# The experts' second product in bfloat16 halves, and expert numbers fetched four at a time

## The reference, cut to what matters

```
logits = einsum('btd,ed->bte', x, Wr); probs = softmax(logits)
topk_vals, topk_idx = top_k(probs, 2)
router_weights = topk_vals / topk_vals.sum(-1)
h = silu(x @ W1[e].T)        # W1: 8 x 512 x 128
y = h @ W2[e].T              # W2: 8 x 128 x 512
out = sum over the two experts of gate * y
```

## Time and profile before

| | |
|---|---|
| median of 3 executions | 565.09 us (564.62 to 568.42) |
| the profiled execution | 566.33 us |
| its span in the trace | 564.5 us |
| first expert stage, hidden(0) to the last outputs | 267.8 to 366.6 us |
| second expert stage | 450.0 to 546.6 us |
| TensorE matmul busy | 488.1 us (86%) |
| VectorE, ScalarE, GpSimd busy | 292.4, 250.6, 247.5 us |

### The profile page before, as it was taken

The page is one execution under the profiler, slowest core; times in us unless marked ns, Lnnn a source line. Parts: engine busy times, 40 slices in busy tenths (PEclk is TensorE's granted clock), DMA queues, the critical chain, the costliest instruction groups (busy, mean ns, idle before and its releaser), DMA issues.

```text
span 564.5 us, 12563 instructions
## 1 busy us (share of the span) xinstructions
PE 488.1 (86%) x4071; PEld 378.0 (67%) x4071; DVE 292.4 (52%) x960; ACT 250.6 (44%) x529; POOL 247.5 (44%) x229
## 2 busy tenths in 40 slices
PE   1989999999999999899979999937998499999970
PEld 0647776868666887766867787715777297787750
DVE  5556495948796789746731010057577743010115
ACT  7754566573645444333322323346663122232333
POOL 7134262435332464641676253621146567343460
PEclk9998898999898999989889999969998679999995
DMA  7865292967396337011132310040001223311007
GB/s 234 255 145 82 61 171 63 171 135 104 86 148 134 66 95 130 15 34 39 39 87 82 82 35 24 36 149 2 1 19 40 66 68 82 86 53 35 21 30 224
DMA packets 66594, 48.36 MB, mean 86 GB/s; under 512 B 7861, under 2 KB 60615, under 8 KB 66534
## 3 DMA queue, kind: packets, MB, share of 16 engines
q1 hardware_dynamic: 61430, 36.99, 30.8%
q0 software_dynamic: 5104, 10.57, 5.3%
HBM read 16.14 MB, written 27.59 MB: 77 GB/s over the span
## 4 chain that ended last, share of the span: by engine, by line
PE 70%; DVE 11%; issue 6%; DMA 5%; POOL 3%; SPq 2%; ACT 2%; POOLq 0%; DVEq 0%; ACTq 0%
PE PS L817 14%; PE PS L658 9%; PE PS L801 7%; PE PS L803 4%; PE PS L645 3%; PE PS L710 3%; PE PS L620 3%; PE PS L802 3%; PE PS L639 3%; PE PS L556 2%; DMA X<-in_x 2%; PE PS L602 2%; PE PS L668 2%; PE PS L629 2%; SPq L303 2%
## 5 line engine op out<-in xcount | busy, mean ns | idle before, releaser
L507 POOL DMA_INDIRECT YY<-W2R,ID x78 | 77.0, 988 | 81.4 <-ACT W2R L1296 62.8
L451 POOL TENSOR_TENSOR R<-NM,I64B 128x1024 bf16<-128x1024 f32 x32 | 61.4, 1920 | 114.0 <-DVE NM L1464 109.0
L1288 ACT ACTIVATE W2R<-PS 128x512 f32<-128x512 f32 x78 | 46.6, 597 | 125.9 <-PE PS L803 125.8
L817 PE MATMUL PS<-WB,W2R 128*128 x624 | 90.5, 291 | 0.0
L495 POOL DMA_INDIRECT XS<-W1R,SLOT x64 | 64.0, 1000 | 48.0 <-DVE SLOT L1590 31.4
L801 PE MATMUL PS<-QKM,WA 128*128 128x128 bf16 x312 | 71.7, 232 | 9.6 <-issue 4.4
L817 PEld LDWEIGHTS PS<-WB,W2R 128*128 128x128 f32 x624 | 77.8, 197 | 2.4 <-issue 0.2
L1741 DVE COPY QKM<-PS 128x1024 bf16<-128x1024 bf16 (+1 forms) x20 | 13.5, 677 | 123.6 <-PE PS L780 123.6
L803 PE MATMUL PS<-QKM,WA 128*128 128x128 bf16 x312 | 71.7, 232 | 0.0
L802 PE MATMUL PS<-QKM,WA 128*128 128x128 bf16 x312 | 69.5, 225 | 0.0
L658 PEld LDWEIGHTS PS<-VB,PF 128*128 128x128 f32 x512 | 60.1, 193 | 9.2 <-issue 9.2
(11 more groups left out here) (207 smaller groups left out, 871.2 us busy)
## 6 DMA issues: line engine op xcount, KB each, us to landing
XS<-CST SPq DMA_DIRECT2D x30, 520.0 KB, 9.9
QKM<-XS SPq DMA_DIRECT2D x78, 65.0 KB
QKM<-QK SPq DMA_DIRECT2D x64, 72.0 KB, 2.1
QKM<-YY SPq DMA_DIRECT2D x16, 256.0 KB, 4.8
W2R<-in_W POOLq DMA_DIRECT2D x1, 2048.0 KB, 12.3
YY<-W2R,ID POOLq DMA_INDIRECT x78, 2.2
XS<-CST SPq DMA_DIRECT2D x2, 585.0 KB, 9.0
XS<-W1R,SLOT POOLq DMA_INDIRECT x64
```

Of the source, the lines that this page charges most:

```text
L451: nc.gpsimd.tensor_tensor(R[:, u % 2], NM[:, u % 2].unsqueeze(2).to_broadcast([P, NH, WIN]), I64B[:].unsqueeze(1).to_broadcast([P, NH, WIN ...
L507: pool.indirect_dma_start(out=YY[f], out_offset=to, in_=YS[n % NY][:, i, :], in_offset=None, bounds_check=NPAIRS - 1, oob_is_err=False) \
L817: last = mm(o, HF[n % 3][:, k, :], WB[:, e, k, :].rearrange("p o c -> p (o c)"), start=k == 0, stop=k == KF - 1)
L1288: fn(HF[n % 3], PS[:, n % 3, :].rearrange("p (k s) -> p k s", k=KF), ACT.Silu).then_inc(s["f_hf"], 1)
```

## The change

The hidden activations are split into a bfloat16 high half and the bfloat16 rest, and the weights WB likewise, as two halves of each 128 columns beside each other. For each of the four k, `outputs(t)` makes one product of the high activations with both halves of the weights (256 columns, the two results beside each other in PSUM), and one of the low activations with the high weights, added onto the first 128 columns. The two halves of the result are added when PSUM is copied out.

- ScalarE's `silu(t)` becomes two: SiLU to float32 (HF, now two buffers) and SiLU again to bfloat16 (high half of HB).
- VectorE gets `low(t)`: HF less the high half, to the low half of HB, for every tile.
- `y_out` moves from ScalarE to VectorE: a sum over pairs of PSUM values 128 columns apart. It runs on 2 tiles at a time, the last three tiles singly, since a bank now holds 2 tiles; YS has 8 buffers of 2 tiles in place of 4 of 4. It is called at the head of `low(t)` for the pair that ended with tile t-2.
- `choose` loads the four expert numbers of a group at once, ahead of the group, and without the instructions that hold the value against its bounds.
- VectorE gets `second_lo(e)` in block A: the low half of each of the eight WB weights, at the end of the units of `W2_STEPS`. What waited for ScalarE's copy to WB now waits for VectorE's.
- In the first stage the sends of the fourth sequence stand behind two pairs of results, in the second still ahead of all.
- `route_gates` on VectorE now stands behind the stage's last `y_out`; `route_table` of the second phase stands behind turned(1) and low(2) in the second stage, where it was ahead of route_place.

```diff
-NY = 4
+NY = 8
...
+YGROUPS = [list(range(g, g + 2)) for g in range(0, NTILE - 3, 2)] + [[g] for g in range(NTILE - 3, NTILE)]
...
-        WB = sb("WB", [P, NE, KF, D])
+        WB = sb("WB", [P, NE, KF, 2, D], BF16)
...
-                    if y == 1 - f:
+                    if y == 2 - 2 * f:
                         dispatch(f, B - 1)
...
-                def choose(t):
+                def choose(g):
+                    tiles = GROUPS[g]
                     for i, (_, t0, _) in enumerate(PHASES):
-                        if t == t0:
+                        if tiles[0] == t0:
                             pe.wait_ge(s["f_table"], 2 * (NPH * f + i + 1))
-                    which[t] = pe.value_load(EID[0:1, t:t + 1], min_val=0, max_val=NE - 1)
+                    _, experts_of = nc.values_load_multi_w_load_instructions(
+                        EID[0:1, tiles[0]:tiles[-1] + 1], engines=[mybir.EngineType.PE], min_val=0, max_val=NE - 1,
...
-                    pe.wait_ge(s["f_hf"], n + 1)
+                    pe.wait_ge(s["f_hl"], n + 1)
...
-                        last = mm(o, HF[n % 3][:, k, :], WB[:, e, k, :].rearrange("p o c -> p (o c)"), start=k == 0,
-                                  stop=k == KF - 1)
+                        hh, hl = (HB[n % 3][:, h, k, :] for h in range(2))
+                        mm(o, hh, WB[:, e, k, :, :].rearrange("p o h c -> p (o h c)"), start=k == 0, stop=False,
+                           skip_group_check=True)
+                        last = mm(o[:, 0:D], hl, WB[:, e, k, 0, :].rearrange("p o c -> p (o c)"), start=False,
+                                  stop=k == KF - 1, skip_group_check=True)
...
                     if t < NTILE and t % 4 == 2 + late and t // 4 + 1 < NGRP:
                         turned(t // 4 + 1)
+                        if not late:
+                            choose(t // 4 + 1)
                     if t >= 2:
                         outputs(t - 2)
-                    if t + 1 < NTILE:
-                        choose(t + 1)
+                    if t < NTILE and t % 4 == 3 and late:
+                        choose(t // 4 + 1)
...
+                    if n >= 2:
+                        act.wait_ge(s["f_hl"], n - 1)
+                    fn(HF[n % 2], z, ACT.Silu).then_inc(s["f_hf"], 1)
                     if n >= 3:
                         act.wait_ge(s["f_y"], n - 2)
-                    fn(HF[n % 3], PS[:, n % 3, :].rearrange("p (k s) -> p k s", k=KF), ACT.Silu).then_inc(s["f_hf"], 1)
...
+                    fn(HB[n % 3][:, 0], z, ACT.Silu).then_inc(s["f_hf"], 1)
...
+            def second_lo(e, bank):
+                dve.wait_ge(s["wt_hi"], NE + e + 1)
+                hi, lo = (WB[:, NE - 1 - e, :, c, :] for c in range(2))
+                v.tensor_tensor(lo, PS[:, bank, :].rearrange("p (k d) -> p k d", d=D), hi, ALU.subtract) \
+                    .then_inc(s["wt_lo"], 1)
...
+                def y_out(*last):
+                    for y in (y for y, tiles in enumerate(YGROUPS) if tiles[-1] in last):
+                        m, w = f * len(YGROUPS) + y, len(YGROUPS[y])
+                        dve.wait_ge(s["f_y"], f * NTILE + YGROUPS[y][-1] + 1)
...
+                        halves = PS[:, 4 + m % 2, 0:2 * w * D].rearrange("p (t h d) -> p t d h", h=2, d=D)
+                        v.tensor_reduce(YS[m % NY][:, 0:w, :], halves, op=ALU.add, axis=AXX).then_inc(s["f_ys"], 1)
+
+                def low(*tiles):
+                    for t in tiles:
+                        n = f * NTILE + t
+                        y_out(t - 2)
+                        dve.wait_ge(s["f_hf"], 2 * n + 2)
+                        if n >= 3:
+                            dve.wait_ge(s["f_y"], n - 2)
+                        v.tensor_tensor(HB[n % 3][:, 1], HF[n % 2], HB[n % 3][:, 0], ALU.subtract).then_inc(s["f_hl"], 1)
...
                 for g in range(3, NGRP):
+                    late = GROUPS[g][0] in [t0 for _, t0, _ in PHASES]
+                    low(*range(4 * g - 4, 4 * g - 2 + late))
                     turned(g)
                     identities(g)
+                    low(*range(4 * g - 2 + late, 4 * g))
```

More of the change, by code:

```diff
@@ L64 @@
 NGRP = len(GROUPS)
-YGROUPS = [list(range(g, g + 4)) for g in range(0, NTILE - 7, 4)] \
-    + [list(range(g, g + 2)) for g in (NTILE - 7, NTILE - 5)] + [[g] for g in range(NTILE - 3, NTILE)]
+YGROUPS = [list(range(g, g + 2)) for g in range(0, NTILE - 3, 2)] + [[g] for g in range(NTILE - 3, NTILE)]
 XROW = D + 2
@@ L249, in program @@
               for c in range(B)]
+        hb = qkm[:, 14592:14592 + 3 * 2 * DFF].rearrange("p (i h k s) -> p i h k s", i=3, h=2, k=KF)
+        HB = [hb[:, i] for i in range(3)]
         w2r = W2R[:].rearrange("p e f -> p (e f)")
         HF = [w2r[:, 512 * i:512 * i + 512].rearrange("p (k s) -> p k s", k=KF) for i in range(3)]
-        YS = [w2r[:, 1536 + 512 * i:1536 + 512 * i + 512].rearrange("p (t d) -> p t d", d=D) for i in range(NY)]
+        YS = [w2r[:, 1536 + 256 * i:1536 + 256 * i + 256].rearrange("p (t d) -> p t d", d=D) for i in range(NY)]
         XR = [XZ[:]] * B, [x[:, 0:2].rearrange("p j k d -> p (j k) d") for x in YL]
@@ L697, in hidden_a @@
                 if f == 1 and b == 0:
-                    pe.wait_ge(s["wt_hi"], NWT)
+                    pe.wait_ge(s["wt_lo"], NWT)
                 if f == 1 and b == 1:
@@ L783, in experts @@
                 which = {}
-                def choose(t):
+                def choose(g):
+                    tiles = GROUPS[g]
                     for i, (_, t0, _) in enumerate(PHASES):
-                        if t == t0:
+                        if tiles[0] == t0:
                             pe.wait_ge(s["f_table"], 2 * (NPH * f + i + 1))
-                    which[t] = pe.value_load(EID[0:1, t:t + 1], min_val=0, max_val=NE - 1)
+                    _, experts_of = nc.values_load_multi_w_load_instructions(
+                        EID[0:1, tiles[0]:tiles[-1] + 1], engines=[mybir.EngineType.PE], min_val=0, max_val=NE - 1,
+                        skip_runtime_bounds_check_because="a count of at most NE experts, clamped to 1 and less 1")
+                    which.update(zip(tiles, experts_of))
                 def hidden(t):
@@ L795, in hidden @@
                     if n >= 3:
-                        pe.wait_ge(s["f_hf"], n - 2)
+                        pe.wait_ge(s["f_hf"], 2 * (n - 2))
                     xh, xl = (FHL[g % 3][:, h, t % 4 * P:t % 4 * P + P] for h in range(2))
@@ L882, in beside @@
                     if c == 1:
-                        pe.wait_ge(s["wt_hi"], NE + 4)
+                        pe.wait_ge(s["wt_lo"], NE + 4)
                     if c >= 3:
@@ L888, in beside @@
                     if c == 1:
-                        pe.wait_ge(s["wt_hi"], NE + 6)
+                        pe.wait_ge(s["wt_lo"], NE + 6)
                     if c >= 2:
@@ L906, in beside @@
                     else:
-                        pe.wait_ge(s["wt_hi"], NE + 1)
+                        pe.wait_ge(s["wt_lo"], NE + 1)
                     select(c + 1, 0, 0, 5)
@@ L911, in beside @@
                     if c == 1:
-                        pe.wait_ge(s["wt_hi"], NE + 7)
+                        pe.wait_ge(s["wt_lo"], NE + 7)
                     if c >= 2:
@@ L1122, in weights_hi @@
                 act.wait_ge(s["wt_ps"], i + 1)
-                o = WB[:, NE - 1 - e].rearrange("p k d -> p (k d)") if second else WA[:, 0, NE - 1 - e, :]
-                fn(o, PS[:, bank, :], ACT.Copy).then_inc(s["wt_hi"], 1)
+                o = WB[:, NE - 1 - e, :, 0, :] if second else WA[:, 0, NE - 1 - e, :].rearrange("p (k d) -> p k d", d=D)
+                fn(o, PS[:, bank, :].rearrange("p (k d) -> p k d", d=D), ACT.Copy).then_inc(s["wt_hi"], 1)
             def padded(dst, src, name, **how):
@@ L1304, in experts @@
                         route_x_t(f, B - 1)
-                    for y, tiles in enumerate(YGROUPS):
-                        if tiles[-1] == t - 2:
-                            y_out(y)
-                for y, tiles in enumerate(YGROUPS):
-                    if tiles[-1] > NTILE - 3:
-                        y_out(y)
                 act.wait_ge(s["f_lg"], (f + 1) * B)
@@ L1691, in beside @@
                     input_variance(c + 2)
+                for e, bank in W2_STEPS.get((c, t), ()):
+                    second_lo(e, bank)
             dve.wait_ge(s["ld_x"], 16)
@@ L1763, in experts @@
                     route_variance(f, c)
+                    low(0)
                     identities(0)
                     route_normalised(f, c)
+                    low(1)
                     route_split(f, c)
                     turned(1)
+                    low(2)
                     identities(1)
                     route_table(f, 1)
+                    low(3)
                     route_choose(f, c)
+                    low(4)
                     route_place(f, c)
+                    low(5)
                     turned(2)
```

(14 more changed lines are left out.)

18 lines of the change are left out of this document (7 added, 11 removed).

## The result

| | before | after |
|---|---|---|
| median of 4 executions each | 564.86 us (561.84 to 568.42) | 546.61 us (545.96 to 553.01) |
| the profiled execution | 566.33 us | 546.39 us |
| its span in the trace | 564.5 us | 544.6 us |
| TensorE, VectorE, ScalarE busy | 488.1, 292.4, 250.6 us | 453.9, 371.5, 275.9 us |

The ratio is 0.97, with an interval of 0.9608 to 0.9792. The change saves 18.25 us of the median and 19.9 us of the span. The prediction's sum was 26.6 us in the trace, a third too large, and its 27 us of the median was half too large. Direction and range held.

The account below looks back on a forecast made before the run. TensorE was taken to set the pace, its instruction queue limiting hidden and its array the outputs. First stage -14.0, second -15.6, block A +3 gave -26.6 us in the trace, hence a 538 us median; range 525 to 553.

Parts of the forecast that it names:

- Steady part: Second expert stage and first alike: a group of four tiles falls from 9.6 to 6.96 us, saving 15.2 and 19.2 us.
- the term for the outputs: Outputs of each tile: counted at 0.54 us by TensorE's queue, though the array needs 0.70; 2.16 us per group.
- The range from 0.30 to 0.84 for a load: Expert-number load on TensorE's queue, once per group: lower bound 0.30 us, upper 0.84, taken as 0.6.
- The array as the bound: Rival for the expert stages: the array, not the queue, limits; a group takes 6.06 us, total 526.5 us; chance 0.12.
- The queue gains nothing: Rival: a k's second product costs the queue 0.12 us, like one with an address; total 560 to 568 us; chance 0.07.
- VectorE as the bound: Rival: sends stretch low to 2.31 us, so VectorE needs 2.9 us a tile; total 599 us; chance 0.05.
- up to double: y_out on VectorE: reading pairs 512 bytes apart might cost up to double the 0.34 us a tile.
- Block A: Eight new VectorE subtractions: three in units 7 to 9, plus waits ahead of them, cost +3 us, bounds 0 and 7.
- The sign that I had named: Block A, unit 9: TensorE's transposes would wait longer for XZ in the changed kernel's profile.
- Heads: Start of each expert stage: later sends cost +1.2 us in the first, outputs(7) waiting for low(7) +3.6 in the second.
- The ends: From last hidden to last send of each stage: old and new paths equal within 0.3 us, counted as 0.

Follow-up runs that it names:

- e1: The kernel before with only the load of four expert numbers at once, float32 outputs and no low or second_lo: 530.08 us, ratio 0.9382.
- e2: The changed kernel with the earlier load, one expert number per tile and with its bounds instructions: 579.5 us, ratio 1.029.
- e5: The kernel before with one load per tile as before, but without its two bounds instructions: 543.31 us, ratio 0.9607.
- e4: The changed kernel with expert 0's first weights for all tiles, so hidden has no address instructions: 529.63 us in one run.
- e3: The changed kernel with each second_lo one unit later on VectorE, behind the next unit's context and maxima: 536.66 us, ratio 0.9507.
- e9: The kernel before with one load per four tiles, the fourth sequence's sends ahead of results, and expert 0's weights in hidden: 523.97 us in one run.
- e8: The changed kernel with second_lo one unit later, low(7) ahead of third-phase route_table, and first-stage fourth-sequence sends ahead of all results: 534.36 us, ratio 0.947.

## Why the prediction was right, and its size wrong

**Steady part: right in kind, 5.9 us too large.** Tiles 16 to 38 were to save 22 x 2.4 x 0.275 = 14.5 us in each stage and saved 11.6 and 11.5. The step that failed is "what the array still has to do while the queue goes on is made up there; I count by the queue, 0.54". Outputs took 0.64, the array's pace, hidden behind them 1.06 in place of 1.02, and transposes and load 0.76 in place of 0.72: 0.40, 0.16 and 0.04 more in a group of four, 0.6 in all, so the term for the outputs is the one that was sized wrong. By the same count the queue had only 0.1 of lead over the array at the end of the outputs, and hidden with its address instructions didn't make it up. Why part of the tiles has a further gap of 0.1 to 0.2 between hidden and outputs isn't settled.

**What the gain comes from: not asked.** The sum took products and load together. By the queue alone the outputs cost 4 x 0.12 = 0.48 in float32 and 0.54 in bfloat16: in that count the products bring nothing, and all of the gain is the load's. The prediction had both numbers and didn't put them beside each other. e1 and e2 show it: 53.0 to 40.7 with the load alone, 53.5 with the products alone. The range from 0.30 to 0.84 for a load was sound, and e5 splits it: 0.31 a tile for the bounds.

**The array as the bound** (rival at 0.12) didn't come true, and e4 shows why: 5.8 us a group, under the 6.06 given, but only without the address instructions of hidden. **The queue gains nothing**: its premise, 0.12 for the second product of a k, is refuted: the weight load of L826 starts 0.01 to 0.07 behind that of L824 in 294 of 312 cases, and four more products a tile cost e2 only 0.02 us a tile (53.5 against 53.0). And yet for the products as such its result is the true one (e2).

The Trainium skill's rule of about 62 ns for every MATMUL with hardware decode off (TensorE: Matmul & The Clock Gate, section Wait — 56ns, not 53.3ns?) would have made a group 9.0 by the prediction's estimate. The trace has 7.5, and in e4 the products of hidden start 0.05 to 0.06 us apart, so that rule doesn't set the pace here. The 0.11 to 0.13 us of a product with an address instruction do: without them in hidden a group falls to 5.8.

**VectorE as the bound** (0.05) is refuted. low and y_out in the change, ns min/median/max:

```profile
L1767 DVE TENSOR_TENSOR QKM<-W2R,QKM x78: 678/682/693, 275.4 to 524.4; 128x512 bf16<-128x512 f32 x78
```

```profile
L1758 DVE TENSOR_REDUCE W2R<-PS x42: 415/691/693, 285.3 to 526.1; 128x256 f32<-128x512 f32 x36, 128x128 f32<-128x256 f32 x6
```

No low was stretched among 78, of which 53 overlap a send in time. In the same trace three of the eight subtractions to HL took 2.30 us in place of 0.73, as in the earlier trace rows. The sum over pairs 512 bytes apart costs 0.69, as the reduce in order of the earlier trace rows, not up to double. By the Trainium skill (SBUF — State Buffer, section Who interferes with whom) a VectorE instruction with two SBUF inputs is held by a GpSimd instruction that reads SBUF; here indirect sends from SBUF didn't hold one.

**Block A: right in kind, too low in size, and mostly elsewhere.** I had +3 from "three subtractions plus the waits ahead of them" in units 7 to 9. e3 puts it at 8 us to unit 17, and the largest waits are elsewhere: six waits of 15.6 us in all, the longest at the end of unit 6, ahead of the maxima of unit 7, the next at the end of unit 13, and only 1.6 us of them at the end of units 7 and 8. The sign that I had named, TensorE waiting longer for XZ, didn't come: that wait of 0.40 us is absent in the change. I priced the instruction, not the wait that the whole of VectorE's list stands behind.

```profile
DVE WB L1406 <- ACT WB L1135: 15.6, 6, 5.4
```

Why the table above has only +4.3: units 17 to 30 took 87.2 us in place of 89.9, at a granted clock of 1.00 in place of 0.97 between 150 and 215 us. That isn't the change's doing, as far as the runs show: e9 has the same 87.2 without second_lo, and e2 88.7 with it. A single trace is a poor measure of this term. hidden(0) of the first stage starts at 263.5 to 269.4 us in the five kernels without second_lo, 266.2 on average, at 263.3 to 265.5 in the three with it later, and at 271.7 to 272.1 in the three with it in its place.

**Heads: right to 2 us.** In the first stage turned(4) was to come at 309.2 and block A's delay later; it came at 311.73 with a block A of 4.3, 1.8 early. The fourth sequence's sends started 3.2 us later against hidden(0) than before, predicted 3.6. TensorE and GpSimd in order of time in the change:

```profile
279.83 0.28 PE L824 MATMUL PS<-WB,QKM 128*128 x1 [1.91 <-DVE QKM L1767]
...
298.80 0.28 PE L824 MATMUL PS<-WB,QKM 128*128 x1 [1.57 <-DVE QKM L1767]
...
311.73 0.62 PE L782 MATMUL PS<-IDENTB,QKM 128*128 128x128 bf16 x8 [1.89 <-DMA QKM<-XS]
...
456.72 0.28 PE L824 MATMUL PS<-WB,QKM 128*128 x1 [2.03 <-DVE QKM L1767]
...
468.37 0.28 PE L824 MATMUL PS<-WB,QKM 128*128 x1 [2.12 <-DVE QKM L1767]
```

```profile
295.75 0.99 POOL L497 DMA_INDIRECT XS<-W1R,SLOT  x1 [0.30 <-issue]
```

In the second stage outputs(7) waits for low(7) behind `route_table`, as predicted; the waits for low at 279.83 (outputs(1)) and 456.72 (outputs(3)) had no term in the sum. What both heads cost shows against e1: hidden(0) to hidden(16) takes 41.2 and 37.8 us in the change, 36.8 and 32.8 in e1. So between these two traces the bfloat16 form costs 9.4 us in the heads, where VectorE's list is full, 1.4 in the steady part, 2.6 ahead of the first hidden(0) and 0.7 in block B and the end, 14.1 in all; the medians of the two differ by 16.5. The 2.6 understates block A, since e1's hidden(0) at 269.4 is the latest of the five kernels without second_lo.

**The ends** came out at +0.9 and +0.5 for 0.

Together: -26.6 predicted, steady part +5.9, heads -1.8, block A +1.3, block B and end +1.4, which gives the -19.8 of the trace.

## What to carry to other kernels

Count each resource apart for each part of a change: where an engine's queue sets the pace, cutting the array's work is worth nothing until the queue's instructions go, and where one change does both, price each alone. A register load for four values cost nearly the same as for one here (0.33 and 0.30 us), and the bounds instructions on it cost as much as the load. In a list in program order, put an instruction that waits for another engine behind what others wait for; its price is the wait, not its length.

## What the runs showed of the hardware

- In hidden the weight load of a product whose address comes from a register starts 0.11 to 0.13 us behind the one before, and that of a product that follows with the same register 0.01 to 0.02. The matmul of the latter still starts 0.06 behind; that its price on the queue is small rests on e2, where four more a tile cost 0.02 us. The array takes a 128-column product in 0.055 (e4). The difference is mostly hidden when slower work (float32 passes, 0.11 to 0.12 each) is on the array just before: 0.055 in e1 with the same address instructions.
- The float32 product of 128 columns takes 0.89 to 0.97 us for four k and its three bfloat16 products 0.63 to 0.66: 0.26 us saved a tile at best (e4 against e9), for an extra SiLU of 0.59, a subtraction of 0.68 and half a reduce.
- With second_lo in its place TensorE was busy 103.0 of 110 us of block A at a mean granted clock of 0.91, where 1.00 is the 2.4 GHz level; one unit later it was busy 108.2 us at 0.98. The clock doesn't follow the busy time alone: the kernel before has 108.9 us at 0.94, e8 106.2 at 0.98. Which part of the 8 us of block A is wait and which is clock wasn't separated. Busy time by engine from 40 to 150 us, the change and then e3:

```profile
40.00:150.00 110.00, 103.03 (x838) 75.90 (x849) 74.83 (x183) 57.63 (x128) 40.88 (x25) 0.91 0.60 104
```

```profile
40.00:150.00 110.00, 108.20 (x927) 77.86 (x925) 79.80 (x204) 63.78 (x145) 43.81 (x27) 0.98 0.57 108
```
